# Two chained convolutions on one core: layer 0's mean computed ahead, layer 1 three chunks behind, one load per image

## The reference

```
x = x + L0(_gn(x))      # L0: depthwise 3x3 conv, then three 64x64 channel mixes
                        # (softmax(A), pointwise P, softmax(G)), all linear, no bias
x = x + L1(_gn(x))      # L1: 3x3 conv of sign(x), weights sign(w)*mean|w| per output channel

def _gn(v, G=32, eps=1e-5):      # 32 groups of two channels
    g = v.reshape(B_, G, C_ // G, H_, W_)
    m = mean(g, (2, 3, 4)); s = var(g, (2, 3, 4))
    return ((g - m) / sqrt(s + eps)).reshape(v.shape)
```

## Time and profile before

| | us |
|---|---|
| median of 3 runs | 2031.15 (2027.94 to 2032.43) |
| the profiled execution | 2029.57 |
| its span, first to last instruction | 2027.7 |
| mean granted TensorE clock | 0.988 |
| TensorE busy | 1860.5 (92%) |
| VectorE busy | 1590.1 (78%) |
| ScalarE busy | 1276.7 (63%) |
| GpSimd busy | 535.9 (26%) |
| HBM read / written | 252.39 MB / 134.22 MB |

### The profile page before, as it was taken

The page is one execution under the profiler, slowest core; times in us unless marked ns, Lnnn a source line. Parts: engine busy times, 40 slices in busy tenths (PEclk is TensorE's granted clock), DMA queues, the critical chain, the costliest instruction groups (busy, mean ns, idle before and its releaser), DMA issues.

```text
span 2027.7 us, 81845 instructions
## 1 busy us (share of the span) xinstructions
PE 1860.5 (92%) x35558; PEld 1553.1 (77%) x35558; DVE 1590.1 (78%) x2508; ACT 1276.7 (63%) x1367; POOL 535.9 (26%) x279
## 2 busy tenths in 40 slices
PE   0099999999999989999899998999899999999876
PEld 0099999999787769777687777777697778999733
DVE  4555567888888887888788887888788888888787
ACT  2145557776667766767577666677567667767554
POOL 0133332322223222223233222233222223223100
PEclk9999999999999999999999998999899999999999
DMA  9933357999899887899798987898878985655466
GB/s 204 194 85 83 83 128 176 228 225 226 214 231 226 225 213 190 224 230 226 181 229 224 229 216 188 227 228 223 215 189 223 230 220 148 156 156 145 105 166 166
DMA packets 315120, 389.10 MB, mean 192 GB/s; under 512 B 23744, under 2 KB 286016, under 8 KB 314944
## 3 DMA queue, kind: packets, MB, share of 16 engines
q1 hardware_dynamic: 314944, 386.70, 76.7%
HBM read 252.39 MB, written 134.22 MB: 191 GB/s over the span
## 4 chain that ended last, share of the span: by engine, by line
PE 80%; DVE 8%; SPq 4%; DMA 3%; issue 3%; ACT 1%; DVEq 0%; ACTq 0%
PE psA L506 69%; PE psB L506 11%; DMA ring<-in_x 3%; SPq L269 3%; DVE ring L884 1%; DVE ring L857 1%; DVE bnt L720 1%; DVE psL L886 1%; DVE pk L869 1%; DVE xc L849 1%; SPq L263 1%; DVE aggr L799 1%; DVE ring L890 1%; ACT rnd L411 1%; ACT xh L385 0%
## 5 line engine op out<-in xcount | busy, mean ns | idle before, releaser
L506 PE MATMUL psA<-xh,W 64*64 64x256 f16 (+1 forms) x19456 | 1633.3, 361 | 41.8 <-issue 30.6
L506 PEld LDWEIGHTS psA<-xh,W 64*64 64x64 f16 x19456 | 1132.5, 107 | 205.0 <-issue 58.6
L506 PE MATMUL psA<-xl,W 64*64 64x512 f16 (+1 forms) x9984 | 1116.9, 361 | 0.0
L321 POOL TENSOR_TENSOR xl<-xc,xn 128x1024 f16<-128x1024 f32 (+2 forms) x264 | 533.0, 2020 | 1315.5 <-ACT xn L381 1315.5
L506 PEld LDWEIGHTS psA<-xl,W 64*64 64x64 f16 x9984 | 622.3, 107 | 79.4 <-issue 0.7
L506 PE MATMUL psB<-pk,W 64*64 64x512 f16 (+3 forms) x5568 | 620.7, 342 | 29.8 <-DVE pk L869 24.7
L381 ACT ACTIVATE xn<-xc 128x1024 f16<-128x1024 f32 (+2 forms) x264 | 272.1, 1034 | 554.1 <-DVE xc L849 554.1
L857 DVE SCALAR_TENSOR_TENSOR ring<-psA,columns,ring 128x1024 f32<-128x1024 f32 x256 | 328.4, 1283 | 295.9 <-PE psA L506 295.9
L385 ACT ACTIVATE xh<-xc 64x1024 f16<-64x1024 f32 (+1 forms) x528 | 543.1, 1032 | 9.3
L506 PEld LDWEIGHTS psB<-pk,W 64*64 64x64 f16 x5568 | 325.5, 106 | 85.3 <-issue 57.3
L720 DVE BATCH_NORM_STATS2 bnt<-ring 128x6 f32<-128x512 f32 x512 | 326.3, 682 | 70.3 <-DMA ring<-in_x 67.9
(11 more groups left out here) (71 smaller groups left out, 99.8 us busy)
## 6 DMA issues: line engine op xcount, KB each, us to landing
ring<-in_x SPq DMA_DIRECT2D x896, 256.0 KB, 4.6
out_y<-ring SPq DMA_DIRECT2D x512, 256.0 KB, 3.5
ring<-in_x SPq DMA_DIRECT2D x32, 512.0 KB, 13.9
pk<-in_w1T SPq DMA_DIRECT2D x2, 144.0 KB, 7.9
rnd<-in_w1n SPq DMA_DIRECT2D x2, 144.0 KB, 7.8
grp<-in_same_group SPq DMA_DIRECT2D x1, 64.0 KB, 6.1
rnd<-in_dw SPq DMA_DIRECT2D x2, 2.2 KB, 5.6
rnd<-in_att SPq DMA_DIRECT2D x1, 16.0 KB, 2.0
```

Of the source, the lines that this page charges most:

```text
L321: ins = nc.gpsimd.tensor_tensor(xl[:, slot:slot + rows, 1:W + 1], xc[:, j:j + rows], xn[:, k:k + rows, 1:W + 1], ALU.subtract)
L506: mm = pe.matmul(bank[out0:out0 + C, c0:c1], weights[src0:src0 + C, :], src[src0:src0 + C, slot:slot + rows, width[0]:width[0] + width[1]] ...
```

## The change

Layer 0 is linear, so the sum over an image of its result can be had from the image before layer 0 is computed: each tap of the depthwise filter sums the normalised image less the row or column that falls off the edge. Six sums per partition do: the whole, the first or last row, the two edge columns, and the corners. VectorE takes the edge columns of each chunk in one more reduction beside bn_stats (`take_borders`), the edge row and corners once an image, and the whole from bn_aggr. With coefficients from the weights (`coef`, `MG`, prepared once) two instructions and the small product on TensorE give the mean. It is ready before layer 0 of the image begins.

Layer 1 then follows 3 chunks behind, LAG = 3, in every image. The ring gets 41 places and holds the next image's chunks, loaded once, 36 ahead of the step; the statistics read them there, 35 ahead. `rnd` has one buffer. `signs` now waits on `a_post`, the add-back of the next chunk. TensorE's loop over images is written out. The spare places, `acc`, `sum_of_x1`, and the early loads go.

```diff
-RING = 39
-SPARE = 2
-AHEAD = 4
-LAG = 33
+RING = 41
+LAG = 3
+BEFORE = 35
...
-        rnd = sb("rnd", [128, 2, G, HW], F32)
+        rnd = sb("rnd", [128, G, HW], F32)
...
+            for g in range(NC, RING):
+                load_chunk(g)
             for t in range(ALL):
+                if RING <= t + RING - LAG - 2 < ALL:
+                    load_chunk(t + RING - LAG - 2)
                 if t > LAG:
                     store_chunk(t - LAG - 1)
-                for part in parts_at(t + 1):
-                    load_part(*part)
-                if NC <= t + AHEAD < ALL:
-                    load_chunk(t + AHEAD)
...
             def signs(img, ch):
                 if ch.at(0):
                     act.wait_ge(mean1_rdy, img + 1)
+                act.wait_ge(a_post, n + 1 if ch.at(NC - 1) else n + 2)
...
             def round_b(img, ch):
                 act.wait_ge(b_mm, n + 1)
-                if n >= 2:
-                    act.wait_ge(y_rdy, n - 1)
+                if n >= 1:
+                    act.wait_ge(y_rdy, n)
...
             for t in range(ALL):                       # ScalarE
-                if t > NC and t % NC != 0:
-                    signs_of(t - NC)
+                if t + 1 >= LAG:
+                    signs_of(t + 1 - LAG)
                 if t + 1 < ALL:
                     high_of(t + 1)
...
-                pe.matmul(psL[:, 1, 0:1], grp[:], st[:, 0:1], start=True, stop=True)
+                pe.matmul(psL[:, 1, 0:1], MG[:], border, start=True, stop=True)
...
+            def step(img, a, between=None):            # TensorE
+                if img == 0 and a < LAG:
+                    step_alone(img, Chunk(0, a), between)
+                elif a < LAG:
+                    step_one(img, Chunk(0, a), img - 1, Chunk(0, a + NC - LAG), between)
                 else:
+                    step_one(img, Chunk(0, a), img, Chunk(0, a - LAG), between)
...
-            with pe.Fori(0, NB - 3) as b:
-                image(b + 2, True)
+            image(0, 2)
+            for img in range(1, NB):
+                image(img, 1)
+            for i in range(NC - LAG, NC):
+                step_signs(NB - 1, Chunk(0, i))
...
+            def take_borders(img, i):                  # VectorE
+                at = place(img, i)
+                here = ring[:, at:at + CE].rearrange("p (s w) -> p w s", s=G)
+                nc.vector.reduce_sum(colp[:, :, i], here[:, 0:W:W - 1, :], AX.X)
+                for edge, (p0, p1), lo in ((0, LO, at), (NC - 1, HI, at + CE - W)):
+                    if i == edge:
+                        nc.vector.reduce_sum(sums[p0:p1, img % 2, 1:2], ring[p0:p1, lo:lo + W], AX.X)
+                        nc.vector.tensor_copy(sums[p0:p1, img % 2, 4:6], ring[p0:p1, lo:lo + W:W - 1])
...
+                nc.vector.tensor_copy(sums[:, img % 2, 0:1], aggr[:, 0:1])      # in stats_parts
+                nc.vector.reduce_sum(sums[:, img % 2, 2:4], colp[:], AX.X)
...
+                steps.link(nc.vector.scalar_tensor_tensor(out=parts6[:, 0, :], in0=counts[:], scalar=mean0[:, 0:1],
+                                                          in1=sums[:, img % 2, :], op0=ALU.mult, op1=ALU.subtract))
+                nc.vector.scalar_tensor_tensor(out=parts6[:, 1, :], in0=parts6[:, 0, :], scalar=rstd0[:, 0:1],
+                                               in1=coef[:], op0=ALU.mult, op1=ALU.mult,
+                                               accum_out=border).then_inc(border_rdy, 1)
...
                 nc.vector.scalar_tensor_tensor(out=here, in0=psA[:, ch.par, :], scalar=osc[:, 0:1], in1=here,
-                                               op0=ALU.mult, op1=ALU.add,
-                                               accum_out=acc[:, ch.i:ch.i + 1]).then_inc(a_post, 1)
+                                               op0=ALU.mult, op1=ALU.add).then_inc(a_post, 1)
...
+                if a == 0:
+                    mean_of_x1(img)
+                if t + 1 >= LAG:
+                    pack(*of(t + 1 - LAG))
```

More of the change, by code:

```diff
@@ L92, in conv_preact @@
     ALL = NB * NC
[L96 to L99, removed]
     def parts_at(t):
-        return [(img, i) for img in (t // NC + 1, t // NC + 2) if img < NB for i in range(NC)
-                if part_step(img, i) == t]
-    EARLY = 3
+        return range(NC, NC + 3) if t == 0 else range(NC + 3, NC + 5) if t == 1 else range(t + BEFORE, t + BEFORE + 1)
     AGGR_STEP, GROUP_STEP, SCALE_STEP = NC - 4, NC - 3, NC - 2
[L108 to L116, removed]
     with ExitStack() as ctx:
@@ L165, in conv_preact @@
         st = sb("st", [128, 12], F32)
-        columns = sb("columns", [128, 9], F32)
-        magic, spare, early, mean0, rstd0, mean1, nmean1, osc, wmean = (columns[:, k:k + 1]
-                                                                                for k in range(9))
+        columns = sb("columns", [128, 10], F32)
+        magic, spare, early, mean0, rstd0, border, nmean_even, nmean_odd, osc, wmean = (columns[:, k:k + 1]
+                                                                                        for k in range(10))
+        nmean1 = (nmean_even, nmean_odd)
         w_in = sem("w_in")
@@ L304, in _ @@
             nc.gpsimd.memset(magic[:], MAGIC).then_inc(pz, 1)
+            for k, count in enumerate((1, W, H // 2, H // 2, 1, 1)):
+                nc.gpsimd.memset(counts[:, k:k + 1], count).then_inc(pz, 1)
             pool.wait_ge(amax_rdy, 1)
@@ L441, in _ @@
                     square_root(t // NC + 1)
[L444 to L448, removed]
+            for g in range(ALL + 1 - LAG, ALL):
+                signs_of(g)
+            for g in range(ALL - LAG, ALL):
                 round_of(g)
@@ L669, in _ @@
             pe.wait_ge(w_rdy, 2)
[L670 to L681, removed]
-                else:
[L683 to L686, removed]
+            pe.wait_ge(pz, 15)
@@ new lines, in step, with image @@
+            def step(img, a, between=None):
[3 more added lines that the diff above has]
+                    step_one(img, Chunk(0, a), img - 1, Chunk(0, a + NC - LAG), between)
+                else:
+                    step_one(img, Chunk(0, a), img, Chunk(0, a - LAG), between)
+            def image(img, first):
+                for i in range(4 * first):
+                    step(img, i, (lambda: mean_average(img)) if i == 0 else None)
+                with pe.Fori(first, NC // 4 - 1) as v:
@@ L696, in _ @@
[L696 to L706, removed]
+                    step(img, i, (lambda: gather_stats(img + 1)) if i == GROUP_STEP and img + 1 < NB else None)
@@ L781, in link, with take_part @@
                     dve.wait_ge(self.sem, self.count)
[L783 to L791, removed]
+            STATS_STEPS = 15
+            def take_part(g):
+                img, i = divmod(g, NC)
+                dve.wait_ge(ld[g % 2], 32 * ld_count(g))
+                take_borders(img, i)
+                at = place(img, i)
                 bn_tuples(ring[:, at:at + CE], i).then_inc(bn_done, 1)
@@ L915, in _ @@
                     add_layer1(*of(t - LAG - 1))
-                for part in parts_at(t):
-                    take_part(*part)
+                for g in parts_at(t):
+                    if g < ALL:
+                        take_part(g)
                 if img + 1 < NB:
```

111 lines of the change are left out of this document (52 added, 59 removed).

## The result

The changed kernel takes 1946.7 us, median of 4 runs (1943.5 to 1947.5), against 2029.97 (4 runs) of the kernel before: a ratio of 0.9586, 95% interval 0.957 to 0.9603. Forecast were 1916.5, with 1892 to 1962. The direction and the range held; 30 us of the expected gain are missing.

A forecast was written before the change was run, and what follows sets the result against it. TensorE was taken to set the step of 6.93 us. From 2029.57 us, start +1.45, longer steps +19.6, borders -35.1 and end -99.0 gave 1916.5, with 1892 to 1962 for 8 in 10.

The forecast's parts named there:

- Layer 1 three chunks behind: 30 steps grow from 6.28 to 6.933 us, +19.6; after the last add-back 16.3 remain of 115.3, -99.0.
- Inside a step, cost 0: Later signs put `xh` at +5.53 us, wanted at +6.93, leaving 1.4 of cover; pack also ends in time.
- Sums of the edges, cost 0: VectorE's edge reduction per chunk takes 0.15 us within 1.06 idle, with no wait for GpSimd.
- Image loop written out: TensorE's four jumps back go with their 4.6 + 3 us stops and low clock; borders in all -35.1.
- The border, 3.2 each: Each of seven image borders loses 3.2 us, bounds 0.5 and 7.1; 22.4 in all instead of 57.5.
- Nothing lost elsewhere: Between steps, only the seven borders lose time; straight code with inner loops of four steps costs no stop.
- Each image loaded once: 117 MB of re-reading go; no bandwidth bound, but DMA waits before the statistics go, -1.37 us per border.
- Rival 3, fetching stays: TensorE's longer program still stops at each border, 7 x 12.4 us instead of 22.4: +64, 1981; chance 8%.
- The signs named ahead: Add-backs every 6.93, last near 1898; border `xh` waits 1 to 3; clock 1.00, no border "issue" stops; about 134 MB read.
- likeliest case: The whole run without any rival: chance 72%, own range 1892 to 1951 us.

The follow-up runs named there:

- e9: The changed kernel with three more ScalarE passes in front of each high part, each waiting for the one before: 2054.4 us, ratio 1.0138.
- e4: The kernel before with one edit, TensorE's loop over images 2 to 6 written out: 1994.0 us, ratio 0.9826.
- e1: The changed kernel with the copy of the two corner values made by a reduction instead: 1926.5 us, ratio 0.9498.
- e2: As e1, with edge row and corners taken in steps 2 and 31 and the border instructions in step 31: 1916.6 us, ratio 0.9457.
- e3: The changed kernel with TensorE's inner loops of four steps written out too: 1986.3 us, ratio 0.9781.
- e8: The changed kernel with one more ScalarE pass over 512 elements in front of each high part, result unused: 1956.9 us, ratio 0.9634.
- e5: The kernel before, reading 58 MB less by leaving out half of the data for the statistics, so its output differs: 2015.2 us, ratio 0.9934.

## Why the prediction came out as it did

- *Layer 1 three chunks behind* (+19.6 and -99.0): right. 30 steps take 6.93 instead of 6.28; the end took 17.7 (16.3), since of the 33 chunks that layer 1 did alone 3 are left. Rounding 254 and 255 alternated with the additions as described.
- *Inside a step, cost 0*: right, to 0.04 us for `xh`. e9 measured the cover that was claimed.
- *Sums of the edges, cost 0*: right for the reduction per chunk, 0.16 (0.15 forecast). The Trainium skill ("SBUF — State Buffer", section "Who interferes with whom") says that tensor_reduce never contends with GpSimd on trn2, and the trace agrees: 0.16 beside a running subtraction.
- *Image loop written out*: right in place, and e4 gives its size, -34.8.
- *The border, 3.2 each*: this step failed; the borders lost 43.5, or 6.2 each. It listed "a copy and a reduction of 64 elements after bn_aggr (0.3), two linked instructions (0.45)", and put the edge row and the corner copy only at the start. The diff takes them for every image, through `take_part` of chunks 31 and 0, and parts_at puts these into steps 28 and 29. They cost 0.33 and 1.1 each time. e1 and e2 take these apart: of the 43.5, 20.0 went with the copy (13.3 held time, 6.5 a clock that stayed up) and 9.1 with the place of the rest; 14.4 are left, 2.1 each, less than the 3.2 forecast.
- *Nothing lost elsewhere*: this failed too, by 9.3. The sentence "straight code with the inner loops of four steps costs no such stop" rested on images 1 and 2 of the kernel before; it doesn't carry further. e3 shows that the inner loops' jumps are not what costs, since without them there are more stops (45.4 outside the borders). What sets the stops off stays open.
- *Why the copy was held*: the trace shows it ending with GpSimd's subtraction. e8 and e9 show that its length follows the subtraction. The same section of the Trainium skill ("SBUF — State Buffer", "Who interferes with whom") says that a copy can enter a 2-port mode and then contends with GpSimd; the traces agree, 1.11 beside it and 0.16 without. The section was read for the reduction alone. A warning was also in hand: the earlier trace rows show a small instruction, though one with two inputs, standing 1.52 beside GpSimd.
- *Each image loaded once* (-1.37 per border): right that late loads go, too small in all (13.5 for half of the bytes, from e5), and one effect was not seen: 8.0 of that were stops of TensorE on "issue", most of them at the jumps. Those go with the jumps, too, so the two gains can't be added.
- *Rival 3, fetching stays*: not at the borders, where it was put; the stops inside images may be of its kind. With more of the code straight they become the larger loss (e3).
- *The signs named ahead*: add-backs every 6.93, HBM reads and the edge reductions came out as said. The last add-back was at 1927.84 and not near 1898, six waits for `xh` were 3.45 and not 1 to 3, and the granted clock fell to 0.83 at four borders, which was named as a sign of being wrong.

The median lies inside the likeliest case's own range (to 1951) because its upper bound had the edge reductions on the path and one instruction held by GpSimd at each border, 7.1 each, and I took the lower middle of it without asking of each edge instruction in which step it runs. That the range held is partly luck: it had no room of its own for the 9.3 elsewhere, and the borders stayed 0.9 each below their bound.

## What to carry to other kernels

Work that comes once per image is free or dear by the step it lands in: list, for each such instruction of the diff, the step of every image in which it runs, and look at what else is there; here moving some 1.4 us of it per border and changing one copy of two numbers took 29 us off the borders. Of each new instruction of VectorE ask whether GpSimd can hold it, the tiny ones too: the copy stood for as long as the subtraction still had to run (1.1 and 1.6 us for 0.15 of work). In this kernel TensorE's program had a best mix of loops: a jump back over a long body cost 5 to 9 us, but straight code all through cost 40; loops over a few steps with short straight pieces between were the fastest.

## What was not expected of the hardware

- A copy of 64 x 2 f32 took 1.11 us at the median and 1.29 at most beside GpSimd (1.6 to 1.8 in e8), 0.15 with no subtraction beside it; the same values by a reduction took 0.14.
- TensorE's program in straight code: 4.65 MB of instruction packets and 38.3 us on issue in 40 waits, at a DMA load of about half.
- TensorE's stop at a jump back over a long body depended on the loads: the first stop of each jump was 4.57 to 4.84 us in the kernel before, 3.26 to 3.47 when 58 MB less were read (e5).
- The granted clock fell at four of seven borders of the changed kernel (0.83 over 10 us, 1.6 us each), behind waits of 3.45. The length of the waits doesn't decide it: in e4 it was 0.83 over 980 to 990, behind one wait of 1.92, and in e8, whose waits for `xh` came to 4.3 per border, the steps behind the first six borders stayed at 7.28. This stays open.
